# A GRU step with the state as the stationary operand and the weights streaming in four column tiles

## The chip, the cores and the metric

The kernel runs on one NeuronCore of a Trainium2 chip. The metric is the device time of one execution in microseconds. TensorE (PE in the profile), VectorE (DVE), ScalarE (ACT), GpSimd (POOL) and SyncE (SP) each run their own instruction stream in order and meet through semaphores.

## The reference

Four graph layers in a row over 1250 nodes with 512 features, each followed by a residual and a layer norm. Nearly everything the change touches is the recurrent part of the first one:

```python
def gru(x_seq, W_ih, W_hh, b_ih, b_hh):
    H = W_hh.shape[1]                       # 512
    pre_i = x_seq @ W_ih.T + b_ih           # [1250, 1536], all steps at once
    def step(h, pi):
        ph = h @ W_hh.T + b_hh              # [1536]
        r = sigmoid(pi[:H] + ph[:H])
        z = sigmoid(pi[H:2 * H] + ph[H:2 * H])
        n = tanh(pi[2 * H:] + r * ph[2 * H:])
        return (1.0 - z) * n + z * h
    # scan over the 1250 rows, h0 = 0; every h is kept
```

Each step needs the whole state of the step before, so 1250 products of a 1x512 vector with a 512x1536 matrix run one after the other.

## The kernel before

**Around the loop.** The program first builds the dense adjacency from the edge lists, runs two graph convolutions, and computes `pre_i` for all steps into `big` (line 952), seen as `pi_v`, 12 columns for each step. After the loop come the output product of this layer and the other three layers. None of that is changed but for the order of the 12 columns.

**Numbers.** State and weights are f16 pairs (high part and low part of a scaled f32), with f32 accumulation in PSUM. `whh16[g]` holds the recurrent weights of gate g (0 r, 1 z, 2 n) as two parts by four k tiles of 128x512. `h16` holds the state: which of two buffers, which half, which k of the half, and two columns (high and low part) for each.

**TensorE (lines 488 to 516).** A matmul has a 128x128 block of weights as the stationary operand and the two state columns as the moving one, so its output is two PSUM columns over 128 partitions. A gate is 4 output blocks x 4 k x 2 parts = 32 matmuls, a step is 96, each with its own weight load. The outputs are in two halves c of 256 features; each half has a PSUM bank for each gate (4c + g). Lines 501 to 516 write the order by hand: what needs only half 0 of the new state goes first (after `gru_state0`), then, after `gru_state1`, what needs half 1, with r, n and z of half 0 ahead of those of half 1. So the gates of one half are worked on by the other engines while TensorE multiplies for the other half.

**ScalarE (lines 688 to 725)** puts the step's input columns into the PSUM banks beside the products (`put`, line 691, six small copies a step) and applies the sigmoids (lines 703 and 708) and the tanh (line 712), each for one half.

**VectorE (lines 986 to 1023).** A scan (`tensor_tensor_scan`, running value times a multiplier plus the next element) over 6 or 8 PSUM elements adds high part, low part and input, undoes the scale, and for n multiplies by r (lines 988 and 994). One scan of 14 elements makes the new state and the pieces for its f16 split (line 1001). Line 1007 writes `h16` and releases TensorE; line 1009 writes the signed copy of the state into `upd_add` for the next update. All of this is per half, so there are two of each in a step.

**GpSimd (line 325)** copies the new state of a half into `r1`, which keeps all 1250. `gru_kept` and `gru_fresh` guard the next overwrite of the buffers.

All loops are written for two steps a turn (u = 0, 1; t = 2i + u).

Of the kernel before, what the change touches and what calls it, by code (L numbers as in the profile page):

```python
# [25 lines left out]
ACT = mybir.ActivationFunctionType  # L26
ALU = mybir.AluOpType
# [6 lines left out]
N, D, E = 1250, 512, 20000  # L34
P = 128
# [14 lines left out]
L2_STEPS = 35  # L50
WSLOT = KT * D


def layout(nc, io):

    ctx = ExitStack()
    with ctx:
# [35 lines left out]
        whh = [r2_f[:, 0:WSLOT], r2_f[:, WSLOT:2 * WSLOT], hn_f[:, WSLOT:2 * WSLOT]]  # L93

# [107 lines left out]
        def _(sp):  # L202
# [44 lines left out]
            for c in range(2):  # L247
                sp.wait_ge(s(f"gru_put{c}"), N + 1)
# [35 lines left out]
        def _(pool):  # L284
# [61 lines left out]
        def _(pe):  # L346
# [139 lines left out]
            every = ((0, 0), (0, 1), (1, 0), (1, 1))  # L486

            def gru_gate(u, c, kc, g, pieces=every):

                for j, k in pieces:  # L490
                    at = (4 if g == 2 else 3) * j
                    for part in range(2):
                        m = mm(psum[:, 4 * c + g, at:at + 2], whh16[g][:, part, 2 * kc + k, (2 * c + j) * P:(2 * c + j + 1) * P],  # L493
                               h16[:, u, kc, k], start=(kc == 0 and j == 0 and k == 0 and part == 0),
                               stop=(kc == 1 and k == 1 and part == 1), skip_group_check=True)
                return m

            with pe.Fori(0, N // 2) as i:
                for u in range(2):
                    t = 2 * i + u  # L500
                    pe.wait_ge(s("gru_state0"), t + 1)
                    pe.wait_ge(s("gru_put0"), t + 1)
                    for g in (0, 2, 1):
                        gru_gate(u, 0, 0, g)
                    pe.wait_ge(s("gru_put1"), t + 1)
                    gru_gate(u, 1, 0, 0)
                    gru_gate(u, 1, 0, 2, every[:1])
                    pe.wait_ge(s("gru_state1"), t + 1)
                    gru_gate(u, 0, 1, 0).then_inc(s("gru_r_mm0"), 1)
                    gru_gate(u, 0, 1, 2).then_inc(s("gru_n_mm0"), 1)  # L510
                    gru_gate(u, 0, 1, 1).then_inc(s("gru_z_mm0"), 1)
                    gru_gate(u, 1, 1, 0).then_inc(s("gru_r_mm1"), 1)
                    gru_gate(u, 1, 0, 2, every[1:])
                    gru_gate(u, 1, 1, 2).then_inc(s("gru_n_mm1"), 1)
                    gru_gate(u, 1, 0, 1)
                    gru_gate(u, 1, 1, 1).then_inc(s("gru_z_mm1"), 1)

            for c in range(2):
                pe.wait_ge(s(f"gru_kept{c}"), N + 2)
                pe.wait_ge(s(f"gru_put{c}"), N + 1)  # L520
# [115 lines left out]
        def _(act):  # L636
# [51 lines left out]
            def put(t, c, g):  # L688

                columns = psum[:, 4 * c + 2, 3:8:4] if g == 2 else psum[:, 4 * c + g, 2:6:3]  # L690
                return nc.scalar.copy(columns, big[:, bass.ds(t * 12 + c * 6 + 2 * g, 2)])  # L691

            for c in range(2):
                for g in range(2):
                    put(0, c, g)
                put(0, c, 2).then_inc(s(f"gru_put{c}"), 1)
            with act.Fori(0, N // 2) as i:
                for u in range(2):
                    t = 2 * i + u

                    def gate_r(c):
                        act.wait_ge(s(f"gru_r_sum{c}"), t + 1)
                        nc.scalar.activation(mul_n[:, c, 3:8:4], sum_rz[:, c, 0, 2:6:3], ACT.Sigmoid).then_inc(s(f"gru_r{c}"), 1)  # L703

                    def gate_z(c):

                        act.wait_ge(s(f"gru_z_sum{c}"), t + 1)
                        nc.scalar.activation(upd_mul[:, c, 2:14:7], sum_rz[:, c, 1, 2:6:3], ACT.Sigmoid).then_inc(s(f"gru_z{c}"), 1)  # L708
# [74 lines left out]
        def _(dve):  # L783
# [174 lines left out]
            link(v.memset(mul_rz[:], 1.0))  # L958
            link(v.memset(mul_rz[:, 0:6:3], 0.0))
            link(v.tensor_copy(mul_rz[:, 2:6:3], scl[:, 1:2].to_broadcast([P, 2])))  # L960
            link(v.memset(mul_n[:], 1.0))
            link(v.memset(mul_n[:, :, 0:8:4], 0.0))
            for c in range(2):
                link(v.tensor_copy(mul_n[:, c, 2:8:4], scl[:, 1:2].to_broadcast([P, 2])))
# [9 lines left out]
            for c in range(2):  # L974
                link(v.memset(psum[:, 4 * c:4 * c + 3, 0:8], 0.0))
                link(v.tensor_copy(psum[:, 4 * c + 2, 2:8:4], bhhc[:, 8 + 2 * c:10 + 2 * c]))
            dve.sem_inc(s("gru_init"), 1)
            for c in range(2):
                dve.sem_inc(s(f"gru_state{c}"), 1)
                dve.sem_inc(s(f"gru_fresh{c}"), 1)  # L980
            signs_v = signs[:].rearrange("p (j a) -> p j a", a=2)

            def sevens(ap):
                return ap.rearrange("p (j a) -> p j a", a=7)

            def scan_rz(t, c, g):
                dve.wait_ge(s(f"gru_{'rz'[g]}_mm{c}"), t + 1)
                v.tensor_tensor_scan(sum_rz[:, c, g], mul_rz[:], psum[:, 4 * c + g, 0:6], 0.0, ALU.mult, ALU.add).then_inc(s(f"gru_{'rz'[g]}_sum{c}"), 1)  # L988

            def scan_n(t, c):  # L990

                dve.wait_ge(s(f"gru_n_mm{c}"), t + 1)
                dve.wait_ge(s(f"gru_r{c}"), t + 1)
                v.tensor_tensor_scan(sum_n[:, c], mul_n[:, c], psum[:, 4 * c + 2, 0:8], 0.0, ALU.mult, ALU.add).then_inc(s(f"gru_n_sum{c}"), 1)  # L994

            def update(t, u, c):
                dve.wait_ge(s(f"gru_kept{c}"), t + 1)
                dve.wait_ge(s(f"gru_fresh{c}"), t + 1)
                for gate in "zn" if c == 0 else "nz":
                    dve.wait_ge(s(f"gru_{gate}{c}"), t + 1)  # L1000
                v.tensor_tensor_scan(upd[:, 1 - u, c], upd_mul[:, c], upd_add[:, c], 0.0, ALU.mult, ALU.add).then_inc(s(f"gru_upd{c}"), 1)  # L1001

            def parts(t, u, c):

                dve.wait_ge(s(f"gru_upd{c}"), t + 1)
                new = sevens(upd[:, 1 - u, c])
                v.tensor_tensor(h16[:, 1 - u, c], new[:, :, 3:6:2], new[:, :, 5:7], ALU.subtract).then_inc(s(f"gru_state{c}"), 1)  # L1007

                v.tensor_tensor(sevens(upd_add[:, c])[:, :, 1:3], new[:, :, 2:3].broadcast_to([P, 2, 2]), signs_v, ALU.mult).then_inc(s(f"gru_fresh{c}"), 1)  # L1009

            with dve.Fori(0, N // 2) as i:
                for u in range(2):
                    t = 2 * i + u
                    scan_rz(t, 0, 0)
                    scan_rz(t, 0, 1)
                    scan_n(t, 0)
                    scan_rz(t, 1, 0)
                    update(t, u, 0)
                    scan_n(t, 1)
                    parts(t, u, 0)  # L1020
                    scan_rz(t, 1, 1)
                    update(t, u, 1)
                    parts(t, u, 1)
# [236 lines left out]
```

## Time and profile before

| | us |
|---|---|
| median of 3 runs | 5472.36 (5461.36 to 5474.08) |
| span of the profiled execution | 5472.0 |
| TensorE matmul busy | 5225.6 (95%) |
| TensorE weight load busy | 4436.6 (81%), beside the matmuls |
| VectorE busy | 2755.6 (50%) |
| ScalarE busy | 2097.4 (38%) |
| GpSimd busy | 611.5 (11%) |
| matmuls and weight loads of line 493 | 120000 of each |

Busy time is the union of an engine's instructions; a small matmul counts from its start until its result is out (about 165 ns here), so overlapping matmuls show a busy engine whatever their rate. The rate is read from the starts. PEclk is the clock granted to TensorE, in tenths of its full 2.4 GHz (1.00 in the tables by stretch is full speed, 0.50 is 1.2 GHz).

### The profile page before, as it was taken

What the parts mean: (1) busy time and instruction counts of PE and PEld (TensorE: products, weight loads), DVE (VectorE), ACT (ScalarE), POOL (GpSimd) and SP (SyncE); (2) the same over time, 40 slices, a digit from 0 to 9 for tenths busy, and PEclk for the clock granted to TensorE, in tenths of its full rate; (3) what the DMA queues carried; (4) which work ended last, traced back from release to release, by engine and by line L of the source; (5) the groups of instructions that cost most, each with busy time, mean ns of one, the idle gap of its engine ahead of it and who ended that gap; (6) DMA issues with size and microseconds to landing.
All of it is one profiled execution on the core that took longest, in us unless ns stands there. A gap on an engine that the chain in (4) does not pass through costs nothing.

```text
span 5472.0 us, 323782 instructions
## 1 busy us (share of the span) xinstructions
PE 5225.6 (95%) x128234; PEld 4436.6 (81%) x128235; DVE 2755.6 (50%) x16453; ACT 2097.4 (38%) x15422; POOL 611.5 (11%) x2721
## 2 busy tenths in 40 slices
PE   8889999999999999999999999999999999999989
PEld 7875569999999999999999999999999744555554
DVE  5552245555555555555555555555555542554451
ACT  0110115555555555555555555555555301211110
POOL 1230001111111111111111111111111100000000
PEclk9999985555555555555555555555555699999999
DMA  1002220000000000000000000000000100000011
GB/s 57 0 9 88 77 85 0 0 0 0 0 0 0 0 0 0 0 0 0 0 0 0 0 0 0 0 0 0 0 0 0 45 10 16 34 33 19 33 40 48
DMA packets 28930, 81.07 MB, mean 15 GB/s; under 512 B 1594, under 2 KB 1834, under 8 KB 28858
## 3 DMA queue, kind: packets, MB, share of 16 engines
q1 hardware_dynamic: 28858, 80.03, 4.0%
q8 instruction: 55, 0.90, 0.1%
q14 instruction: 17, 0.14, 0.0%
HBM read 58.08 MB, written 21.95 MB: 15 GB/s over the span
## 4 chain that ended last, share of the span: by engine, by line
PE 69%; DVE 14%; ACT 7%; issue 7%; DVEq 3%; POOL 0%; DMA 0%; SPq 0%; POOLq 0%; ACTq 0%
PE psum L493 40%; PE psum L555 8%; ACT upd_mul L708 5%; PE psum L372 5%; DVE sum_rz L988 4%; DVE sum_n L994 4%; PE psum L362 4%; PE psum L567 4%; PE psum L419 4%; DVE h L1007 3%; ACT upd_add L712 2%; PE psum L479 2%; PE psum L541 2%; PE psum L631 1%; DVE upd L1001 1%
## 5 line engine op out<-in xcount | busy, mean ns | idle before, releaser
L493 PE MATMUL psum<-h,r 128*128 128x2 f16 x80000 | 2949.1, 166 | 119.8 <-ACT psum L691 4.9
L493 PEld LDWEIGHTS psum<-h,r 128*128 128x128 f16 x80000 | 2613.0, 105 | 223.9 <-DVE h L1007 218.3
L493 PE MATMUL psum<-h,hn 128*128 128x2 f16 x40000 | 1758.5, 165 | 0.2 <-issue 0.2
L493 PEld LDWEIGHTS psum<-h,hn 128*128 128x128 f16 x40000 | 1453.4, 104 | 0.3 <-issue 0.3
L988 DVE TENSOR_TENSOR_SCAN sum_rz<-mul_rz,psum 128x6 f32<-128x6 f32 x5000 | 833.8, 167 | 823.3 <-PE psum L493 823.1
L703 ACT ACTIVATE mul_n<-sum_rz 128x2 f32<-128x2 f32 x2500 | 517.5, 207 | 1409.4 <-DVE sum_rz L988 1409.4
L691 ACT COPY psum<-big 128x2 f32 (+1 forms) x7506 | 1027.7, 159 | 0.0
L1001 DVE TENSOR_TENSOR_SCAN upd<-upd_mul,upd_add 128x14 f32<-128x14 f32 x2500 | 467.0, 187 | 769.0 <-ACT upd_mul L708 460.5
L325 POOL COPY r<-upd 128x2 f32 x2500 | 469.0, 188 | 3224.8 <-DVE upd L1001 3224.8
L708 ACT ACTIVATE upd_mul<-sum_rz 128x2 f32<-128x2 f32 x2500 | 516.2, 206 | 212.4 <-DVE sum_rz L988 199.0
L712 ACT ACTIVATE upd_add<-sum_n 128x2 f32<-128x2 f32 x2500 | 495.9, 198 | 72.5 <-DVE sum_n L994 0.3
L1007 DVE TENSOR_TENSOR h<-upd 128x4 f16<-128x4 f32 x2500 | 409.9, 164 | 43.3
L994 DVE TENSOR_TENSOR_SCAN sum_n<-mul_n,psum 128x8 f32<-128x8 f32 x2500 | 423.6, 169 | 0.1
L1009 DVE TENSOR_TENSOR upd_add<-upd,signs 128x4 f32<-128x4 f32 x2500 | 391.7, 157 | 0.0
L419 PE MATMUL psum<-r 125*125 125x100 bf16 x2580 | 307.2, 309 | 16.5 <-DVE r L863 12.6
L419 PEld LDWEIGHTS psum<-r 125*125 125x125 bf16 x2580 | 286.8, 225 | 32.8 <-DVE r L863 29.0
L372 PE MATMUL psum<-adj,hn 125*128 125x417 f32 (+1 forms) x720 | 252.7, 512 | 2.1 <-ACT hn L656 1.4
L372 PEld LDWEIGHTS psum<-adj,hn 125*128 125x128 f32 x720 | 135.7, 189 | 119.6 <-issue 115.0
L555 PE MATMUL psum<-adj,r 128*125 128x512 f16 x960 | 220.7, 388 | 8.3 <-DVE r L1186 8.3
L862 DVE TENSOR_SCALAR r<-r,hn 125x1250 bf16<-125x1250 f16 x258 | 141.1, 547 | 161.8 <-issue 99.0
L555 PEld LDWEIGHTS psum<-adj,r 128*125 128x125 f16 x960 | 133.4, 139 | 89.6 <-issue 16.1
L362 PE MATMUL psum<-ws,r 128*125 128x512 f32 x400 | 181.6, 617 | 7.2 <-ACT r L730 5.9
(233 smaller groups left out, 2635.0 us busy)
## 6 DMA issues: line engine op xcount, KB each, us to landing
ws<-in_Wl SPq DMA_DIRECT2D x9, 1024.0 KB, 5.4
ws<-in_Wr SPq DMA_DIRECT2D x9, 1024.0 KB, 8.3
edge_counts<-adj SPq DMA_DIRECT2D x2, 3051.8 KB
edge_weights<-big SPq DMA_DIRECT2D x1, 6103.5 KB
adj_rows<-big SPq DMA_DIRECT2D x1, 6103.5 KB
adj<-adj_rows SPq DMA_DIRECT2D x1, 6103.5 KB
big<-edge_counts SPq DMA_DIRECT2D x1, 6103.5 KB
adj<-edge_weights SPq DMA_DIRECT2D x1, 6103.5 KB
```

The costliest lines, as they stand in the source:

```text
L372: m = mm(o[:, 0:n1 - n0], rows[0:NP, t, f * P:(f + 1) * P], mat[0:NP, t, n0:n1], start=(t == 0), stop=(t == NT - 1))
L419: m = mm(psum[0:NP, 2 * u + t // 5, (t % 5) * 100:(t % 5) * 100 + 100], src_hot[0:EP, h, t * NP:(t + 1) * NP], dst_hot[0:EP, h], start=Fal ...
L493: m = mm(psum[:, 4 * c + g, at:at + 2], whh16[g][:, part, 2 * kc + k, (2 * c + j) * P:(2 * c + j + 1) * P], h16[:, u, kc, k], start=(kc == ...
L555: m = mm(o, a(pa), b(pb), start=start and i == 0, stop=stop and i == 2)
L691: return nc.scalar.copy(columns, big[:, bass.ds(t * 12 + c * 6 + 2 * g, 2)])
L703: nc.scalar.activation(mul_n[:, c, 3:8:4], sum_rz[:, c, 0, 2:6:3], ACT.Sigmoid).then_inc(s(f"gru_r{c}"), 1)
L708: nc.scalar.activation(upd_mul[:, c, 2:14:7], sum_rz[:, c, 1, 2:6:3], ACT.Sigmoid).then_inc(s(f"gru_z{c}"), 1)
L712: nc.scalar.activation(upd_add[:, c, 0:14:7], sum_n[:, c, 3:8:4], ACT.Tanh).then_inc(s(f"gru_n{c}"), 1)
L988: v.tensor_tensor_scan(sum_rz[:, c, g], mul_rz[:], psum[:, 4 * c + g, 0:6], 0.0, ALU.mult, ALU.add).then_inc(s(f"gru_{'rz'[g]}_sum{c}"), 1)
L994: v.tensor_tensor_scan(sum_n[:, c], mul_n[:, c], psum[:, 4 * c + 2, 0:8], 0.0, ALU.mult, ALU.add).then_inc(s(f"gru_n_sum{c}"), 1)
L1001: v.tensor_tensor_scan(upd[:, 1 - u, c], upd_mul[:, c], upd_add[:, c], 0.0, ALU.mult, ALU.add).then_inc(s(f"gru_upd{c}"), 1)
L1007: v.tensor_tensor(h16[:, 1 - u, c], new[:, :, 3:6:2], new[:, :, 5:7], ALU.subtract).then_inc(s(f"gru_state{c}"), 1)
```

## The change

The operands of the recurrent matmuls trade places. The two state columns of a k tile become the stationary operand (a weight load of 2 columns), and the weights become the moving one, 128 columns a matmul. The output is two rows (high and low part of the state). Four matmuls that differ only in j write to PSUM partitions 32j and 32j + 1, each in its own column tile of 32 columns of the array, with the same state and a quarter of the gate's weights each: moving column (b, i) of tile j is output feature 128b + 32j + i. A gate is 4 k x 2 parts x 4 tiles = 32 matmuls into one bank, a step 96 as before.

The result lies in rows, and the rest of the step wants it in columns. So VectorE turns the bank with one transpose of 32x32 blocks (128 columns from PSUM) into `turned` in SBUF, four blocks of 34 entries a gate, in reversed order so that the two wanted rows land next to entries 32 and 33, where the n bias and the input stand. A scan then covers two blocks, 38 elements, most of them multiplied by zero. There are two scans a gate.

The halves are gone: one wait for the whole state, then r, n, z; one transpose and two scans for each gate; one activation for each gate over four blocks; one update scan of 28 elements; one subtraction for `h16`. `put` is one copy of 12 elements into the other buffer of `turned`, after z's sigmoid. The signed copy into `upd_add` moves from VectorE to GpSimd, ahead of the keeping copy, which now covers all four blocks.

```diff
+QR = 32
+GRP = QR + 2
+SPAN = GRP + 4
...
+        turned = hn_f[:, 2 * WSLOT:2 * WSLOT + 6 * KT * GRP].rearrange("p (u g b e) -> p u g b e", u=2, g=3, b=KT)
...
             with pool.Fori(0, N // 2) as i:
                 for u in range(2):
                     t = 2 * i + u
-                    for c in range(2):
-                        pool.wait_ge(s(f"gru_upd{c}"), t + 1)
-                        pool.tensor_copy(r1[:, 2 * c:2 * c + 2, bass.ds(t, 1)], upd[:, 1 - u, c, 2:14:7]).then_inc(s(f"gru_kept{c}"), 1)
+                    pool.wait_ge(s("gru_upd"), t + 1)
+                    new = upd[:, 1 - u].rearrange("p c (j a) -> p (c j) a", a=7)
+                    pool.tensor_tensor(upd_add[:].rearrange("p c (j a) -> p (c j) a", a=7)[:, :, 1:3], new[:, :, 2:3].broadcast_to([P, KT, 2]),
+                                       signs[:, 0:2].unsqueeze(1).broadcast_to([P, KT, 2]), ALU.mult).then_inc(s("gru_fresh"), 1)
+                    pool.tensor_copy(r1[:, :, bass.ds(t, 1)], new[:, :, 2:3]).then_inc(s("gru_kept"), 1)
...
-            def gru_gate(u, c, kc, g, pieces=every):
...
+            def gru_rows(u, g):
+
+                for k in range(KT):
                     for part in range(2):
+                        for j in range(4):
+                            w = whh16[g][:, part, k].rearrange("p (b j i) -> p b j i", j=4, i=QR)[:, :, j]
+                            o = psum[QR * j:QR * j + 2, g, 0:KT * QR].rearrange("p (b i) -> p b i", i=QR)
+                            m = mm(o, h16[:, u, k // 2, k % 2], w, start=(k == 0 and part == 0), stop=(k == KT - 1 and part == 1), skip_group_check=True)
                 return m
...
+                    pe.wait_ge(s("gru_state"), t + 1)
+                    gru_rows(u, 0).then_inc(s("gru_r_mm"), 1)
+                    gru_rows(u, 2).then_inc(s("gru_n_mm"), 1)
+                    gru_rows(u, 1).then_inc(s("gru_z_mm"), 1)
...
+            def put(t, u):
+
+                return nc.scalar.copy(turned[:, u].rearrange("p g b e -> p (g b) e")[:, :, QR + 1], big[:, bass.ds(t * 12, 12)])
...
+                    act.wait_ge(s("gru_r_sum"), 2 * t + 2)
+                    nc.scalar.activation(mul_n[:, :, 3:SPAN:GRP], sum_rz[:, :, 0, 3:SPAN:GRP], ACT.Sigmoid).then_inc(s("gru_r"), 1)
+                    act.wait_ge(s("gru_n_sum"), 2 * t + 2)
+                    nc.scalar.activation(upd_add[:, :, 0:14:7], sum_n[:, :, 3:SPAN:GRP], ACT.Tanh).then_inc(s("gru_n"), 1)
+                    act.wait_ge(s("gru_z_sum"), 2 * t + 2)
+                    nc.scalar.activation(upd_mul[:, :, 2:14:7], sum_rz[:, :, 1, 3:SPAN:GRP], ACT.Sigmoid).then_inc(s("gru_z"), 1)
+                    put(t + 1, 1 - u).then_inc(s("gru_put"), 1)
...
+            def turn_rows(t, u, g):
+                gate = "rzn"[g]
+                dve.wait_ge(s(f"gru_{gate}_mm"), t + 1)
+                v.transpose(turned[:, u, g, :, QR - 1::-1], psum[:, g, 0:KT * QR].rearrange("p (b i) -> p b i", i=QR)).then_inc(s(f"gru_{gate}_turned"), 1)
+
+            def gate_span(u, c, g):
+                at = 2 * c * GRP + QR - 2
+                return turned[:, u, g].rearrange("p b e -> p (b e)")[:, at:at + SPAN]
 
             with dve.Fori(0, N // 2) as i:
                 for u in range(2):
                     t = 2 * i + u
+                    turn_rows(t, u, 0)
+                    dve.wait_ge(s("gru_put"), t + 1)
+                    dve.wait_ge(s("gru_r_turned"), t + 1)
+                    for c in range(2):
+                        v.tensor_tensor_scan(sum_rz[:, c, 0], mul_rz[:], gate_span(u, c, 0), 0.0, ALU.mult, ALU.add).then_inc(s("gru_r_sum"), 1)
+                    turn_rows(t, u, 2)
+                    dve.wait_ge(s("gru_n_turned"), t + 1)
+                    dve.wait_ge(s("gru_r"), t + 1)
+                    for c in range(2):
+                        v.tensor_tensor_scan(sum_n[:, c], mul_n[:, c], gate_span(u, c, 2), 0.0, ALU.mult, ALU.add).then_inc(s("gru_n_sum"), 1)
+                    turn_rows(t, u, 1)
+                    dve.wait_ge(s("gru_z_turned"), t + 1)
+                    for c in range(2):
+                        v.tensor_tensor_scan(sum_rz[:, c, 1], mul_rz[:], gate_span(u, c, 1), 0.0, ALU.mult, ALU.add).then_inc(s("gru_z_sum"), 1)
+                    dve.wait_ge(s("gru_kept"), t + 1)
+                    dve.wait_ge(s("gru_fresh"), t + 1)
+                    dve.wait_ge(s("gru_z"), t + 1)
+                    dve.wait_ge(s("gru_n"), t + 1)
+                    v.tensor_tensor_scan(upd[:, 1 - u].rearrange("p c a -> p (c a)"), upd_mul[:].rearrange("p c a -> p (c a)"),
+                                         upd_add[:].rearrange("p c a -> p (c a)"), 0.0, ALU.mult, ALU.add).then_inc(s("gru_upd"), 1)
+                    dve.wait_ge(s("gru_upd"), t + 1)
+                    new = upd[:, 1 - u].rearrange("p c (j a) -> p (c j) a", a=7)
+                    v.tensor_tensor(h16[:, 1 - u].rearrange("p c k a -> p (c k) a"), new[:, :, 3:6:2], new[:, :, 5:7], ALU.subtract).then_inc(s("gru_state"), 1)
```

## Rows read from the trace of the kernel before

**Rows 1.** The span in 40 slices: busy tenths of TensorE, and its granted clock.
```profile
PE   8889999999999999999999999999999999999989
PEclk9999985555555555555555555555555699999999
```

**Rows 2.** The chain of work that ended last, shares of the span by line.
```profile
PE psum L493 40%; PE psum L555 8%; ACT upd_mul L708 5%; PE psum L372 5%; DVE sum_rz L988 4%; DVE sum_n L994 4%; PE psum L362 4%; PE psum L567 4%; PE psum L419 4%; DVE h L1007 3%; ACT upd_add L712 2%; PE psum L479 2%; PE psum L541 2%; PE psum L631 1%; DVE upd L1001 1%
```

**Rows 3.** By stretch: length, engines' busy us (instructions), granted clock, DMA share, GB/s.
```profile
200.00:300.00 100.00, 85.01 (x713) 79.80 (x713) 57.22 (x131) 15.81 (x30) 31.11 (x45) 1.00 0.00 0
...
792.00:4333.00 3541.00, 3424.53 (x119924) 3320.96 (x119921) 1907.30 (x14996) 1847.40 (x14997) 469.02 (x2500) 0.50 0.00 0
...
5328.00:5340.00 12.00, 6.10 (x23) 3.77 (x22) 6.89 (x20) 3.15 (x6) 2.74 (x5) 0.50 0.32 131
```

**Rows 4.** Timeline of one step: start us, length us, engine, line, idle before.
```profile
2002.76 0.29 PEld L493 LDWEIGHTS psum<-h,r 128*128 128x128 f16 x8 [0.17 <-DVE h L1007]
2002.91 0.21 ACT L708 ACTIVATE upd_mul<-sum_rz 128x2 f32<-128x2 f32 x1
...
2003.24 0.19 DVE L1001 TENSOR_TENSOR_SCAN upd<-upd_mul,upd_add 128x14 f32<-128x14 f32 x1 [0.37 <-ACT upd_mul L708]
2003.47 0.17 DVE L1007 TENSOR_TENSOR h<-upd 128x4 f16<-128x4 f32 x1
...
2003.90 0.17 PE L493 MATMUL psum<-h,r 128*128 128x2 f16 x1
...
2004.10 0.17 DVE L988 TENSOR_TENSOR_SCAN sum_rz<-mul_rz,psum 128x6 f32<-128x6 f32 x1 [0.40 <-PE psum L493]
...
2004.30 0.21 ACT L703 ACTIVATE mul_n<-sum_rz 128x2 f32<-128x2 f32 x1 [1.13 <-DVE sum_rz L988]
...
2004.53 0.17 DVE L988 TENSOR_TENSOR_SCAN sum_rz<-mul_rz,psum 128x6 f32<-128x6 f32 x1 [0.26 <-PE psum L493]
...
2004.61 0.17 DVE L994 TENSOR_TENSOR_SCAN sum_n<-mul_n,psum 128x8 f32<-128x8 f32 x1
...
2004.91 0.50 PEld L493 LDWEIGHTS psum<-h,r 128*128 128x128 f16 x16
...
2005.59 0.10 PEld L493 LDWEIGHTS psum<-h,r 128*128 128x128 f16 x1 [0.17 <-DVE h L1007]
```

**Rows 5.** Groups of the loop: count, busy us, mean ns of one, idle before.
```profile
L493 PEld LDWEIGHTS psum<-h,r 128*128 128x128 f16 x80000 | 2613.0, 105 | 223.9 <-DVE h L1007 218.3
...
L988 DVE TENSOR_TENSOR_SCAN sum_rz<-mul_rz,psum 128x6 f32<-128x6 f32 x5000 | 833.8, 167 | 823.3 <-PE psum L493 823.1
L703 ACT ACTIVATE mul_n<-sum_rz 128x2 f32<-128x2 f32 x2500 | 517.5, 207 | 1409.4 <-DVE sum_rz L988 1409.4
L691 ACT COPY psum<-big 128x2 f32 (+1 forms) x7506 | 1027.7, 159 | 0.0
L1001 DVE TENSOR_TENSOR_SCAN upd<-upd_mul,upd_add 128x14 f32<-128x14 f32 x2500 | 467.0, 187 | 769.0 <-ACT upd_mul L708 460.5
L325 POOL COPY r<-upd 128x2 f32 x2500 | 469.0, 188 | 3224.8 <-DVE upd L1001 3224.8
...
L1007 DVE TENSOR_TENSOR h<-upd 128x4 f16<-128x4 f32 x2500 | 409.9, 164 | 43.3
L994 DVE TENSOR_TENSOR_SCAN sum_n<-mul_n,psum 128x8 f32<-128x8 f32 x2500 | 423.6, 169 | 0.1
```

**Rows 6.** Line 1007: shortest, median and longest ns, first and last start us.
```profile
L1007 DVE TENSOR_TENSOR h<-upd x2500: 149/164/166, 792.4 to 4332.5; 128x4 f16<-128x4 f32 x193
```

**Rows 7.** Timeline of TensorE: a run of f16 matmuls of 512 columns.
```profile
4774.78 17.21 PE L555 MATMUL psum<-adj,r 128*125 128x512 f16 x79
```

**Rows 8.** VectorE copies out of PSUM, by shape.
```profile
L902 DVE COPY big<-psum 125x500 f32<-125x500 f32 x20 | 12.5, 665 | 90.0 <-PE psum L461 90.0
...
L902 DVE COPY big<-psum 125x250 f32<-125x250 f32 x10 | 4.0, 404 | 0.0
```

**Rows 9.** Line 401: weight loads of a single column.
```profile
L401 PEld LDWEIGHTS psum<-ident,hn x4: 76/98/119, 11.5 to 11.6; 50*1 50x1 f32 x4
```

More of the change, by code:

```diff
@@ L316, in _ @@
             pool.partition_all_reduce(wmax[:, 7:8], wmax[:, 6:7], P, bass.bass_isa.ReduceOp.max).then_inc(s("top_all"), 1)
-            for c in range(2):
-                pool.sem_inc(s(f"gru_kept{c}"), 2)
+            pool.sem_inc(s("gru_kept"), 2)
             with pool.Fori(0, N // 2) as i:
@@ L500, in _ @@
                     t = 2 * i + u
[L501 to L520, printed above, removed]
+                    pe.wait_ge(s("gru_state"), t + 1)
+                    gru_rows(u, 0).then_inc(s("gru_r_mm"), 1)
+                    gru_rows(u, 2).then_inc(s("gru_n_mm"), 1)
+                    gru_rows(u, 1).then_inc(s("gru_z_mm"), 1)
+            pe.wait_ge(s("gru_kept"), N + 2)
             pe.wait_ge(s("wfc_in"), 16)
@@ L686, in _ @@
             nc.scalar.activation(warm[:], scl[:, 1:2], ACT.Sigmoid).then_inc(s("warm"), 1)
[L688 to L696, printed above, removed]
+            def put(t, u):
+                return nc.scalar.copy(turned[:, u].rearrange("p g b e -> p (g b) e")[:, :, QR + 1], big[:, bass.ds(t * 12, 12)])
+            put(0, 0).then_inc(s("gru_put"), 1)
             with act.Fori(0, N // 2) as i:
@@ L957, in _ @@
             link(v.memset(h16[:], 0.0))
[L958 to L962, printed above, removed]
+            link(v.memset(turned, 0.0))
+            link(v.memset(mul_rz[:], 0.0))
+            link(v.memset(mul_n[:], 0.0))
+            for at in (1, 3):
+                link(v.memset(mul_rz[:, at:SPAN:GRP], 1.0))
+            link(v.memset(mul_n[:, :, 1:SPAN:GRP], 1.0))
+            link(v.tensor_copy(mul_rz[:, 2:SPAN:GRP], scl[:, 1:2].to_broadcast([P, 2])))
             for c in range(2):
-                link(v.tensor_copy(mul_n[:, c, 2:8:4], scl[:, 1:2].to_broadcast([P, 2])))
+                link(v.tensor_copy(mul_n[:, c, 2:SPAN:GRP], scl[:, 1:2].to_broadcast([P, 2])))
+            for u in range(2):
+                link(v.tensor_copy(turned[:, u, 2, :, QR], bhhc[:, 8:12]))
             link(v.memset(upd_mul[:], 1.0))
@@ L973, in _ @@
             link(v.memset(signs[:, 0:4:2], -1.0))
-            for c in range(2):
-                link(v.memset(psum[:, 4 * c:4 * c + 3, 0:8], 0.0))
-                link(v.tensor_copy(psum[:, 4 * c + 2, 2:8:4], bhhc[:, 8 + 2 * c:10 + 2 * c]))
+            link(v.memset(psum[:, 0:6, 0:KT * QR], 0.0))
             dve.sem_inc(s("gru_init"), 1)
[L978 to L1009, printed above, removed]
+            dve.sem_inc(s("gru_state"), 1)
```

51 lines of the change are left out of this document (7 added, 44 removed).

## The prediction

> **What bounds the kernel now.** I read the 40 slices first. From about 0.8 ms to 4.3 ms TensorE is 90% busy or more, and its granted clock is half of full speed [rows 1]. This is the GRU loop, 3541 us of 5472.0 [rows 3], and the chain of work that ended last goes mostly through its matmul line 493 [rows 2]. The diff touches only this loop and its setup, so the rest, 5472.0 - 3541 = 1931 us, stays.
>
> The 2500 operations of line 1007 (two per step) start from 792.4 to 4332.5 us [rows 6]: 3540.1 / 1249.5 = 2.833 us per step. The timeline of one step shows how it fills [rows 4]. Sixteen weight loads of 104 ns each take 0.50 us, so one starts every (0.50 - 0.104) / 15 = 0.0264 us [rows 4, 5]. A step has 96 pairs of weight load and matmul. TensorE waits once a step for the first half of the new state, 0.17 us from the end of the load before [rows 4]; from start to start that is 0.17 + 0.104 = 0.27, of which 0.25 is beyond the pace. (2.833 - 0.25) / 96 = 0.0269. I use 0.0267, between the two: 96 x 0.0267 = 2.56 us. So the step is bound by TensorE, by the rate at which 128x128 weights enter the array. ScalarE, VectorE and the rest of the chain lie almost wholly under it, because the two halves of the state alternate.
>
> **The change, part by part.** The number of pairs stays 96 (3 gates x 4 k x 2 parts x 4 column tiles), but the weight load now has 2 columns and the matmul streams 128. The halves are gone, so everything between the last matmul of the z gate and the first of the next step is exposed. The step is TensorE's time plus that tail.
>
> *TensorE.* No row has two column tiles at work. At full clock, 79 f16 matmuls of 512 columns take 17.21 us, last one 0.39: 0.216 us each, 0.421 ns per column [rows 7]. So 128 columns take 54 ns at 2.4 GHz and 107 ns at 1.2 GHz. Floor: four tiles side by side, a pair every 107 / 4 = 26.7 ns at 1.2 GHz, or 54 / 4 = 13.5 at 2.4. Ceiling: one after the other, 107 or 54 ns a pair. The nearest row for the issue of pairs is the loop itself, 26.7 ns a pair [rows 4, 5]; no row shows a shorter one. I take 26.7 ns, which is both what four tiles give at 1.2 GHz and what is shown to issue: 96 x 0.0267 = 2.56 us, no gain over now.
>
> *The clock.* With 2 moving columns a matmul it stayed at 0.50 through the loop [rows 3]. It was 1.00 where line 419 streams 100 columns a matmul with gaps, and 0.50 in a late stretch where TensorE is busy only half the time [rows 3]. The new loop streams 128 columns and idles for 1.8 us a step, between these two, so either level is possible. With 26.7 ns a pair set by issue, it changes the matmul's own latency only (-0.05 us a step, -65 us in all).
>
> *The tail,* link by link. A link is one start to the dependent start.
> - Last matmul to VectorE: 0.203 now (2003.90 to 2004.10) [rows 4], plus 126 more columns at 1.2 GHz, 0.105: 0.308 (0.256 at 2.4).
> - New 32x32 transpose of 128 elements from PSUM. Copies from PSUM take 404 ns at 250 elements and 665 at 500 [rows 8], 1.044 ns an element plus 143, so 277 at 128. Bounds 0.277 to 0.404; I take 0.30, near the copy and a little up for filling the block. To its reader, as from line 1001 to 1007 (0.22 less 0.187) [rows 4, 5]: 0.035. Sum 0.335.
> - Two scans of 38 elements in place of 6. 6, 8 and 14 elements take 167, 169 and 187 ns [rows 5], 1.3 to 2.9 ns an element: 0.208 to 0.256, I take 0.235. The second starts 0.08 after the first for short ones [rows 4]; with 30 more elements 0.125 to 0.175, I take 0.14. Sum 0.375.
> - VectorE to ScalarE 0.034 (2004.10 to 2004.30 less 0.167), sigmoid 0.206 [rows 4, 5]: 0.240. One activation now covers four blocks; 2 more elements cost nothing visible.
> - Sigmoid end to the update scan: 2002.91 + 0.206 to 2003.24 [rows 4]: 0.13. It waits on four semaphores.
> - Update scan of 28 elements instead of 14: 187 + 14 x (1.3 to 2.9) = 0.205 to 0.227, with its link 0.035: 0.250.
> - State subtraction (0.164 [rows 5], four more elements) and the first load after it: 0.18.
>
> Sum 0.308 + 0.335 + 0.375 + 0.240 + 0.13 + 0.250 + 0.18 = 1.818 us. The step is 2.56 + 1.82 = 4.38 us. The loop grows by (4.38 - 2.833) x 1250 = 1934 us, the kernel to 5472 + 1934 = 7406, rounded 7400. With all links at their ends the step lies between 4.22 and 4.55, so 7200 to 7620. The span equals the median of the runs (5472.36), so nothing is added.
>
> *What costs nothing.* r and n on VectorE: r's matmuls end at 0.85, its transpose can start at 1.16 and its scans end at 1.87, before n's matmuls have arrived at 2.01; n's scans end near 2.7, and z's transpose waits for z's matmuls until 2.87. Cover left 0.15 us; if it is gone, the tail grows by the excess. The input columns: six ScalarE copies of 0.159 a step become one of 12 elements behind z's sigmoid [rows 5]; it needs to land only before the next step's r scans, over a microsecond later. VectorE waits for it ahead of r's scans, with n's transpose queued behind. GpSimd now issues the signed copy of the state (was VectorE's, line 1009) and then the keeping copy (0.188 [rows 5]); both have until the next update, 4 us away. If VectorE's subtraction beside them were slowed by sharing memory ports, up to 0.2 us a step would come on the tail. Setup (a few memsets, other strides for the inputs) runs once: under 5 us.
>
> *Against the skill.* The loop shows a weight load every 26.7 ns beside matmuls in flight [rows 4, 5]. The Trainium skill (TensorEngine Tiling (Array Packing), Instruction Overhead) gives each matmul about 60 cycles however few its columns. As an estimate, that is 25 ns at 2.4 GHz: by it the loop's matmuls would need 2.4 us, not 2.56, even at the high clock, and the 13.5 ns rival below could not occur. I keep that rival at a lower chance.
>
> **Rivals.**
> - *B, high clock and fast issue.* If the clock rises and pairs issue every 13.5 ns, a gate takes 0.43 us and TensorE 1.28. Then VectorE's own in-order chain binds: r arrives at 0.68, its sigmoid ends at 1.63, n's scans start at 1.73, z's transpose at 2.01, its scans end at 2.72, sigmoid and wait to 3.09, update and state to 3.52. Step 3.52: 5472 + 0.687 x 1250 = 6330. For: the 26.7 ns of now is the pace of 128-column loads, not proven to be the issue's. Against: no row issues faster.
> - *C, weight loads come on top.* Four tiles run together, but each round of four also pays its small load. One-column loads show 76 to 119 ns, median 98 [rows 9]. A round is 54 + 98 = 152 ns at 2.4 GHz: 24 rounds 3.65, plus a tail of about 1.77, step 5.4, 8700 us; at 1.2 GHz a round of 205 ns gives a step of 6.74, 10350. For: no row shows small loads beside matmuls in column tiles. Against: loads hide under matmuls everywhere in this trace [rows 4]. The Trainium skill (TensorE: Matmul & The Clock Gate, The mechanism, in the part on packing small matmuls) says a load overlaps a matmul in flight only where the row groups differ, and all four tiles here share theirs; today's loop, with the same row groups throughout, does not bear it out.
> - *D, the change does not do what it says.* The tiles are not concurrent: 96 x 54 ns = 5.18 us, plus 1.77, step 6.95: 5472 + 4.12 x 1250 = 10620 at 2.4 GHz; at 1.2 GHz 10.27 + 1.82 gives 17040. For: nothing here shows concurrency. Against: nothing either, the outputs go to disjoint partitions.
> - *E, faster.* VectorE is the place: B's issue rate, and VectorE's links overlap as short ones do now (0.08 apart) instead of ending first. The step beats 2.833 only if 0.69 us leaves B's chain, which has two exposed transposes and two scan pairs on it: all four at 0.18 instead of 0.335 and 0.375 takes 0.70 away. With 0.1 more from the waits the step is 2.72: 5330 us. Against: a dependent operation waits for its producer's end in every row here.
>
> **How the numbers follow.** A 0.52 (7400; 7200 to 7620), B 0.20, C 0.12 (0.08 of it at the high clock), D 0.12, E 0.03, no change 0.01. The range from 6200 to 8900 takes in A, B and C at the high clock: 0.80. A measurement of this kernel can tell about 0.3% from no change; slower by more has 0.96, within 0.01, faster 0.03. The sign is firm because even the best TensorE leaves a serial chain above 2.833 us.
>
> **What the profile will show.** The loop should last 1250 x 4.38 = 5475 us. If TensorE is right, a gate's 32 matmuls span 0.85 us and TensorE then idles 1.8 us less the latency of its last matmul. B shows gates of 0.43 us, a clock of 1.00 and VectorE at the end of the chain throughout; C about 0.15 or 0.2 us between rounds of four; D gates of 1.7 or 3.4 us. The transposes should take 0.28 to 0.40 us, the scans 0.21 to 0.26. I am wrong if TensorE's gates don't keep to the pace of 26.7 ns a pair, or if VectorE is no longer idle when z's matmuls arrive.

## The result, and the profile after

The changed kernel takes 6795.86 us (median of 4 runs, 6793.9 to 6800.4); the kernel before takes 5469.49 in the same comparison. The ratio is 1.2432, 95% interval 1.2416 to 1.2447: slower, by 1326 us. The profiled execution has a span of 6794.0 us.

The page of the changed kernel, in 40 slices, answers [rows 1]. Busy tenths of TensorE and VectorE, and the granted clock:

```profile
PE   8899744444444444444444444444444448999998
DVE  5542455555555555555555555555555555254552
PEclk9999988888888888888888888888888889989999
```

TensorE is no longer busy for most of the loop, and its clock reads 0.8 where it was 0.5. Neither level of the clock is 0.8. By stretch (length; PE, PEld, DVE, ACT, POOL busy; granted clock), against [rows 3]:

```profile
792.00:5653.00 4861.00, 2344.46 (x119840) 2057.84 (x119828) 2841.58 (x13735) 918.26 (x4996) 415.72 (x2496) 0.81 0.00 0
...
2995.00:3005.00 10.00, 6.34 (x252) 5.62 (x240) 5.93 (x28) 1.68 (x9) 0.67 (x4) 0.52 0.00 0
3007.00:3021.00 14.00, 5.88 (x384) 5.13 (x372) 8.47 (x42) 2.91 (x16) 1.00 (x6) 1.00 0.00 0
```

The loop went from 3541 to 4861 us; the other stages stayed. Inside it, stretches at full clock follow stretches at half clock. So there are two kinds of step. From the starts of the state's subtraction, 897 steps take 3.69 us and 352 take 4.42. Against 2.833 that is 897 x 0.856 + 352 x 1.582 = 1325 us, the whole difference.

One step at half clock, in the timeline (start, length, engine, line, idle before), to be read against [rows 4]:

```profile
3002.42 0.73 PEld L498 LDWEIGHTS psum<-r,h 128*2 128x2 f16 x32 [1.98 <-DVE h L983]
3002.42 1.02 PE L498 MATMUL psum<-r,h 128*2 128x128 f16 x32 [1.69 <-DVE h L983]
3003.12 0.89 PEld L498 LDWEIGHTS psum<-hn,h 128*2 128x2 f16 x32
...
3003.50 0.32 DVE L952 STREAM_TRANSPOSE hn<-psum 128x128 f32<-128x128 f32 x1 [1.13 <-PE psum L498]
...
3003.98 0.88 PEld L498 LDWEIGHTS psum<-r,h 128*2 128x2 f16 x32
3004.08 1.07 PE L498 MATMUL psum<-r,h 128*2 128x128 f16 x32
...
3004.70 0.36 DVE L970 TENSOR_TENSOR_SCAN sum_n<-mul_n,hn 128x38 f32<-128x38 f32 x2
...
3005.21 0.32 DVE L952 STREAM_TRANSPOSE hn<-psum 128x128 f32<-128x128 f32 x1
3005.56 0.36 DVE L974 TENSOR_TENSOR_SCAN sum_rz<-mul_rz,hn 128x38 f32<-128x38 f32 x2
3005.95 0.21 ACT L691 ACTIVATE upd_mul<-sum_rz 128x4 f32<-128x4 f32 x1 [0.64 <-DVE sum_rz L974]
...
3006.36 0.22 DVE L979 TENSOR_TENSOR_SCAN upd<-upd_mul,upd_add 128x28 f32<-128x28 f32 x1 [0.44 <-ACT upd_mul L691]
3006.61 0.17 DVE L983 TENSOR_TENSOR h<-upd 128x8 f16<-128x8 f32 x1
...
3006.84 0.43 PEld L498 LDWEIGHTS psum<-r,h 128*2 128x2 f16 x32 [1.98 <-DVE h L983]
```

Gates follow each other at 0.86 us (3003.12 to 3003.98), 26.7 ns a pair. n's scans are done at 3005.06, z's matmuls end at 3005.15, z's transpose starts at 3005.21: VectorE has been waiting for TensorE. From there to the next step's first load (3006.84) nothing overlaps: 1.69 us.

And one step at full clock:

```profile
3014.22 0.43 PEld L498 LDWEIGHTS psum<-r,h 128*2 128x2 f16 x32 [2.37 <-DVE h L983]
...
3014.61 0.48 PEld L498 LDWEIGHTS psum<-hn,h 128*2 128x2 f16 x32
...
3014.89 0.32 DVE L952 STREAM_TRANSPOSE hn<-psum 128x128 f32<-128x128 f32 x1 [0.72 <-PE psum L498]
3015.05 0.48 PEld L498 LDWEIGHTS psum<-r,h 128*2 128x2 f16 x32
3015.11 0.62 PE L498 MATMUL psum<-r,h 128*2 128x128 f16 x32
3015.31 0.37 DVE L965 TENSOR_TENSOR_SCAN sum_rz<-mul_rz,hn 128x38 f32<-128x38 f32 x2
3015.59 0.29 DVE L952 STREAM_TRANSPOSE hn<-psum 128x128 f32<-128x128 f32 x1
3015.71 0.21 ACT L687 ACTIVATE mul_n<-sum_rz 128x4 f32<-128x4 f32 x1 [2.06 <-DVE sum_rz L965]
3016.02 0.36 DVE L970 TENSOR_TENSOR_SCAN sum_n<-mul_n,hn 128x38 f32<-128x38 f32 x2
3016.30 0.29 DVE L952 STREAM_TRANSPOSE hn<-psum 128x128 f32<-128x128 f32 x1
3016.41 0.21 ACT L689 ACTIVATE upd_add<-sum_n 128x4 f32<-128x4 f32 x1 [0.50 <-DVE sum_n L970]
...
3017.02 0.21 ACT L691 ACTIVATE upd_mul<-sum_rz 128x4 f32<-128x4 f32 x1 [0.40 <-DVE sum_rz L974]
```

A gate takes 0.44 us (3014.61 to 3015.05), 13.9 ns a pair. z's matmuls are done at 3015.73, but VectorE comes to z's transpose only at 3016.30, 0.57 us later. TensorE is not what the step waits for any more, except for the r gate at its start. From r's transpose on it is VectorE's work in order, with one wait in it for ScalarE: n's transpose ends at 3015.88, r's sigmoid at 3015.92, and n's scans start at 3016.02.

### The profile page after: what moved, and what is told of

Read it like the earlier page. It is cut to its first block, busy times and chain, and to the rows that moved or that the text cites. A ratio compares the mean times of both kernels' runs of the same rounds, so it can differ in the third digit from the quotient of the medians.

```text
span 6794.0 us, 302521 instructions
## 1 busy us (share of the span) xinstructions
PE 4145.8 (61%) x128234; PEld 3175.1 (47%) x128235; DVE 3694.9 (54%) x15204; ACT 1168.0 (17%) x5417; POOL 558.8 (8%) x2721
## 4 chain that ended last, share of the span: by engine, by line
issue 72%; PE 19%; POOL 5%; DVE 2%; POOLq 1%; DVEq 1%; ACT 0%; DMA 0%; SPq 0%; ACTq 0%
PE psum L544 6%; POOL r L330 3%; PE psum L556 3%; PE psum L424 3%; PE psum L367 2%; POOL upd_add L328 2%; PE psum L530 1%; PE psum L377 1%; PE psum L620 1%; POOLq L330 1%; POOLq L323 1%; DVE r L830 0%; PE psum L434 0%; DVEq L823 0%; DVEq L822 0%
## 5 line engine op out<-in xcount | busy, mean ns | idle before, releaser
L498 PE MATMUL psum<-r,h 128*2 128x128 f16 x80000 | 1879.0, 247 | 2523.3 <-DVE h L983 2517.0
L498 PEld LDWEIGHTS psum<-r,h 128*2 128x2 f16 x80000 | 1405.5, 95 | 2810.6 <-DVE h L983 2803.6
L952 DVE STREAM_TRANSPOSE hn<-psum 128x128 f32<-128x128 f32 x3750 | 1143.8, 305 | 1120.6 <-PE psum L498 1048.4
L498 PE MATMUL psum<-hn,h 128*2 128x128 f16 x40000 | 933.6, 245 | 0.0
L498 PEld LDWEIGHTS psum<-hn,h 128*2 128x2 f16 x40000 | 747.1, 96 | 0.0
L687 ACT ACTIVATE mul_n<-sum_rz 128x4 f32<-128x4 f32 x1250 | 262.5, 210 | 2713.5 <-DVE sum_rz L965 2713.5
L979 DVE TENSOR_TENSOR_SCAN upd<-upd_mul,upd_add 128x28 f32<-128x28 f32 x1250 | 270.9, 217 | 553.9 <-ACT upd_mul L691 553.9
L970 DVE TENSOR_TENSOR_SCAN sum_n<-mul_n,hn 128x38 f32<-128x38 f32 x2500 | 455.8, 224 | 134.9
L965 DVE TENSOR_TENSOR_SCAN sum_rz<-mul_rz,hn 128x38 f32<-128x38 f32 x2500 | 456.7, 225 | 128.5
L974 DVE TENSOR_TENSOR_SCAN sum_rz<-mul_rz,hn 128x38 f32<-128x38 f32 x2500 | 455.7, 223 | 42.5
L691 ACT ACTIVATE upd_mul<-sum_rz 128x4 f32<-128x4 f32 x1250 | 262.7, 210 | 583.7 <-DVE sum_rz L974 583.7
```

What stands on the lines that cost most here:

```text
L498: m = mm(o, h16[:, u, k // 2, k % 2], w, start=(k == 0 and part == 0), stop=(k == KT - 1 and part == 1), skip_group_check=True)
L691: nc.scalar.activation(upd_mul[:, :, 2:14:7], sum_rz[:, :, 1, 3:SPAN:GRP], ACT.Sigmoid).then_inc(s("gru_z"), 1)
L952: v.transpose(turned[:, u, g, :, QR - 1::-1], psum[:, g, 0:KT * QR].rearrange("p (b i) -> p b i", i=QR)).then_inc(s(f"gru_{gate}_turned"), 1)
L965: v.tensor_tensor_scan(sum_rz[:, c, 0], mul_rz[:], gate_span(u, c, 0), 0.0, ALU.mult, ALU.add).then_inc(s("gru_r_sum"), 1)
L970: v.tensor_tensor_scan(sum_n[:, c], mul_n[:, c], gate_span(u, c, 2), 0.0, ALU.mult, ALU.add).then_inc(s("gru_n_sum"), 1)
L974: v.tensor_tensor_scan(sum_rz[:, c, 1], mul_rz[:], gate_span(u, c, 1), 0.0, ALU.mult, ALU.add).then_inc(s("gru_z_sum"), 1)
```

## The experiments

Three questions were open. Do the four column tiles really run together? What does the clock cost, and what does VectorE's chain? And which part of the change loses the time: the swap of the operands, or the end of the overlap between the halves? All loops below start at about 0.79 ms and the rest of the kernel is unchanged, so a step is read from the subtraction's starts.

**One column tile for all four.**

```diff
-                            o = psum[QR * j:QR * j + 2, g, 0:KT * QR].rearrange("p (b i) -> p b i", i=QR)
+                            o = psum[0:2, g, 0:KT * QR].rearrange("p (b i) -> p b i", i=QR)
```

> The changed kernel, but the four matmuls of a round all use column tile 0 and write the same two PSUM rows (each overwrites or adds to the others, so three quarters of each gate are lost). Counts and shapes of all instructions stay. Theory 1, four column tiles stream side by side and only the streamed columns set the pace: a gate's 32 matmuls now take 32 x 54 = 1.7 us at full clock, the step 5.2 + 1.8 = 7.0 us, the kernel about 10600 us (17000 at half clock). Rival, the pace is that of issuing or of small weight loads and the tiles don't matter: gate and time unchanged, about 6800 us.

Measured: 10918 us (one run). Line 498 in the timeline:

```profile
3001.08 1.76 PEld L498 LDWEIGHTS psum<-r,h 128*2 128x2 f16 x32 [1.86 <-DVE h L983]
...
3002.81 1.81 PEld L498 LDWEIGHTS psum<-hn,h 128*2 128x2 f16 x32
...
3004.59 1.81 PEld L498 LDWEIGHTS psum<-r,h 128*2 128x2 f16 x32
```

A gate takes 1.78 us (3002.81 to 3004.59), 55.6 ns a pair, at a clock of 1.00 throughout, and the step 7.19 us. In four tiles the same pairs take 13.9 ns: the tiles run side by side, at a quarter of the time to within 1%. My rival D (10620 us at full clock) would have looked like this.

**32 streamed columns instead of 128.**

```diff
-                            w = whh16[g][:, part, k].rearrange("p (b j i) -> p b j i", j=4, i=QR)[:, :, j]
-                            o = psum[QR * j:QR * j + 2, g, 0:KT * QR].rearrange("p (b i) -> p b i", i=QR)
+                            w = whh16[g][:, part, k].rearrange("p (b j i) -> p b j i", j=4, i=QR)[:, 0:1, j]
+                            o = psum[QR * j:QR * j + 2, g, 0:QR].rearrange("p (b i) -> p b i", i=QR)
```

> The changed kernel with 32 streamed columns a matmul in place of 128 (three of four feature blocks are left out), same count of pairs. It shows how fast pairs can be issued. If streamed columns alone set the pace, a round of four starts every 27 ns at half clock or 13 at full, and a gate takes 0.21 or 0.11 us; if a pair needs 13.4 ns to issue, a gate keeps 0.43 us; if 26.7 ns, 0.85 us. Theory, VectorE's in-order chain binds once TensorE is fast: the step loses only what the r gate loses, 3.69 - 0.22 = 3.47 us, the kernel about 6270 us. Rival, TensorE's gates still bind: the step loses 0.65 us or more, below 5750 us. The granted clock should be 0.50 throughout if it goes by streamed columns.

Measured: 6303 us (one run), step 3.50 us. By stretch, and in the timeline:

```profile
800.00:5168.00 4368.00, 1213.79 (x119808) 1049.09 (x119808) 2763.97 (x13729) 917.43 (x4992) 415.08 (x2496) 0.50 0.00 0
```

```profile
3002.50 0.25 PEld L498 LDWEIGHTS psum<-r,h 128*2 128x2 f16 x32 [2.66 <-DVE h L983]
...
3002.68 0.36 PEld L498 LDWEIGHTS psum<-hn,h 128*2 128x2 f16 x32
...
3002.98 0.32 DVE L952 STREAM_TRANSPOSE hn<-psum 128x128 f32<-128x128 f32 x1 [0.54 <-PE psum L498]
```

Two things follow. The n gate's 32 loads of 0.079 us take 0.36 us, so a pair is issued every (0.36 - 0.079) / 31 = 9 ns; the r gate's, right behind the wait for the state, come every (0.25 - 0.079) / 31 = 5.5 ns. The n gate's 0.32 us (3002.68 to 3003.00) lies between the values that I had named, 0.21 and 0.43. All this is at half clock; no run shows how close pairs come at full clock. The 26.7 ns of the kernel before was not a pace of issue. And at half clock, with three quarters of TensorE's streaming gone, the step is only 0.19 us shorter than the changed kernel's at full clock. That is the r gate alone: from the first load to r's transpose 0.48 us (3002.50 to 3002.98) instead of 0.67 (3014.22 to 3014.89). VectorE's chain binds, as the theory had it (6270 expected). The clock stayed at 0.50 in the whole loop.

**Filler matmuls behind the z gate.**

```diff
                     gru_rows(u, 1).then_inc(s("gru_z_mm"), 1)
+                    for _ in range(2):
+                        gru_rows(u, 1, 7)
```

(The third argument is the bank.)

> The changed kernel with 64 more matmuls after the z gate (the z gate twice more, into a bank that nobody reads), in the time in which TensorE waits for the state. Theory, the half-speed stretches (352 of 1249 steps at 4.41 us beside 897 at 3.69) come from TensorE idling, and cost 352 x 0.72 = 253 us: granted clock 1.00 through the loop, every step 3.69 us, the kernel 6544 us. Rival, the clock goes by something else: it still alternates, and the time is 6796 us or, where the filler at half clock (1.7 us) delays the next step, more.

Measured: 6539.88 us (ratio to before 1.1961, interval 1.1941 to 1.1981). All 1249 steps take 3.69 us, and the clock stays up:

```profile
800.00:5400.00 4600.00, 2993.96 (x199272) 2760.77 (x199262) 2760.07 (x13701) 917.77 (x4983) 414.82 (x2492) 1.00 0.00 0
```

TensorE is busy 65% of this stretch (2994 of 4600), against 42% in the full-clock stretch of the changed kernel (5.88 of 14 us), which ended in a fall to half clock. The half-clock steps cost 6796 - 6540 = 256 us, where 253 was expected. The rival, a clock that still alternates, did not come.

**The kernel before, whole gates.** TensorE's part of the edit; the others follow the same order.

```diff
                     pe.wait_ge(s("gru_put0"), t + 1)
+                    pe.wait_ge(s("gru_put1"), t + 1)
+                    pe.wait_ge(s("gru_state1"), t + 1)
                     for g in (0, 2, 1):
...
+                        for c in range(2):
+                            gru_gate(u, c, 0, g)
+                            gru_gate(u, c, 1, g).then_inc(s(f"gru_{'rzn'[g]}_mm{c}"), 1)
```

> The kernel before with its operands as they were (weights stationary), but without the overlap of the halves: TensorE waits for both halves of the state, then does the whole r, n and z gates, and the other engines take both halves of each gate one after the other. Theory, the loss of the change is the loss of the overlap: TensorE 2.56 us plus an exposed tail of 0.20 + 0.25 + 0.34 + 0.13 + 0.31 + 0.25 = 1.5 us, step 4.0 us, the kernel about 6950 us, slower than the changed one. Rival, the swap of operands (transposes, long scans) is what costs: then without the halves this kernel stays near its old time, at most 0.3 us a step more, below 5850 us.

Measured: 6721.36 us (ratio 1.2294, interval 1.2273 to 1.2314). The step is 3.84 us, all at half clock:

```profile
3001.37 0.94 PEld L493 LDWEIGHTS psum<-h,r 128*128 128x128 f16 x32 [1.19 <-DVE h L999]
...
3002.23 0.93 PEld L493 LDWEIGHTS psum<-h,hn 128*128 128x128 f16 x32
...
3003.09 0.93 PEld L493 LDWEIGHTS psum<-h,r 128*128 128x128 f16 x32
```

The same 26.7 ns a pair as before, and from the last load's end to the next step's first 1.19 us in which TensorE has nothing to do. This kernel has neither transposes nor long scans nor column tiles, and still loses 1.01 us a step (3.84 - 2.833), nearly all that the change loses (1.06 on average). The rival is excluded. My terms add to 2.56 + 1.48 = 4.04 us, 0.20 too long, nearly all of it in the tail (3.84 - 2.56 = 1.28 us beside the matmuls). It is 75 us faster than the changed kernel, not slower.

**Order r, z, n and early waits.** VectorE's part (the order changes on all three engines):

```diff
+                    dve.wait_ge(s("gru_kept"), t + 1)
+                    dve.wait_ge(s("gru_fresh"), t + 1)
+                    dve.wait_ge(s("gru_r"), t + 1)
+                    turn_rows(t, u, 2)
+                    dve.wait_ge(s("gru_z"), t + 1)
+                    dve.wait_ge(s("gru_n_turned"), t + 1)
...
+                    dve.wait_ge(s("gru_n"), t + 1)
```

> The changed kernel in the order r, z, n in place of r, n, z on all engines, and with the update's waits for GpSimd and for z moved ahead of n's scans, so that only the wait for the tanh stands before the update scan. Same instructions. Theory: the wait for r's sigmoid before n's scans (0.08 us) goes at full clock because z's transpose and scans lie there, and the link from ScalarE to the update shrinks from 0.20 us (end of sigmoid to start of update scan) to about 0.04, at either clock. Steps 3.45 us at full clock and 4.25 at half; with the same share of slow steps about 6530 us. Rival, the waits are not worth anything in themselves: only the 0.08 us of 900 steps, about 6720 us.

Measured: 6522.07 us, the median of four runs of 6468, 6502, 6542 and 6586 us; the ratio, 1.1904 (1.1848 to 1.196), is that of the first three. In the profiled execution (6467.8) 1060 steps take 3.49 us and 189 take 4.42. So the full-clock step lost 0.20 us (0.24 expected), but the half-clock step nothing, where 0.16 was expected; the kernel's time came out near the forecast because fewer steps were slow (189, not 352). The sum was right for a wrong reason.

The end of a half-clock step shows where the gain went:

```profile
3005.68 1.07 PE L498 MATMUL psum<-hn,h 128*2 128x128 f16 x32
...
3006.90 0.32 DVE L952 STREAM_TRANSPOSE hn<-psum 128x128 f32<-128x128 f32 x1 [0.23 <-PE psum L498]
3007.32 0.36 DVE L977 TENSOR_TENSOR_SCAN sum_n<-mul_n,hn 128x38 f32<-128x38 f32 x2
3007.72 0.21 ACT L691 ACTIVATE upd_add<-sum_n 128x4 f32<-128x4 f32 x1 [0.81 <-DVE sum_n L977]
...
3007.96 0.22 DVE L979 TENSOR_TENSOR_SCAN upd<-upd_mul,upd_add 128x28 f32<-128x28 f32 x1 [0.28 <-ACT upd_add L691]
```

The last link is 0.24 us (3007.72 to 3007.96), where the changed kernel has 0.41 (3005.95 to 3006.36): 0.17 gained. But the last gate's matmuls end at 3006.75 and its transpose starts 0.15 us later, where it was 0.06, and its scans follow 0.42 us after that, where it was 0.35: 0.16 lost. At half clock the last transpose waits for TensorE, so the waits moved in front of it and of its scans lie on the path again. At full clock VectorE comes late to that transpose, and what stands in front of it adds nothing: the link to the update gives 0.17; the middle gate's scans start about 0.10 earlier behind their transpose (0.32 us in place of 0.43), no longer waiting for r's sigmoid; the last scans give back 0.07 (0.39 in place of 0.32). Together that is 0.20.

The four runs differ by the clock: their mean granted clocks over the whole execution are 0.921, 0.908, 0.896 and 0.881, from the shortest to the longest. Why the share of half-clock steps varies so much here, and hardly in the changed kernel (0.860 or 0.861 in all four runs), no run shows.

**The same with the filler.** The 64 matmuls stand behind n, now the last gate.

> The order and the early waits, and the 64 filler matmuls behind the last gate. Theory: every step at full clock, 3.45 us, the kernel 1931 + 4313 = 6245 us, still 14% slower than the kernel before, since VectorE's chain (three transposes, six scans, update, subtraction) and not TensorE sets the step. Rival: TensorE is late too, and then the order brings nothing beyond the filler: 6540 us.

Measured: 6288.51 us, ratio 1.1508 (1.1492 to 1.1525), step 3.49 us. The end of a step:

```profile
3003.70 0.29 DVE L954 STREAM_TRANSPOSE hn<-psum 128x128 f32<-128x128 f32 x1
3003.82 0.21 ACT L691 ACTIVATE upd_mul<-sum_rz 128x4 f32<-128x4 f32 x1 [0.40 <-DVE sum_rz L971]
3004.10 0.36 DVE L979 TENSOR_TENSOR_SCAN sum_n<-mul_n,hn 128x38 f32<-128x38 f32 x2
3004.50 0.21 ACT L693 ACTIVATE upd_add<-sum_n 128x4 f32<-128x4 f32 x1 [0.46 <-DVE sum_n L979]
...
3004.74 0.22 DVE L981 TENSOR_TENSOR_SCAN upd<-upd_mul,upd_add 128x28 f32<-128x28 f32 x1 [0.28 <-ACT upd_add L693]
```

From the last activation to the update scan it is again 0.24 us (3004.50 to 3004.74) in place of 0.41: 0.17 us for the place of three of the four waits. The clock is 1.00 from 800 to 5150 us (expected: 3.45 us a step, 6245 us), and the rival, 6540, is excluded. This is the fastest form with the operands swapped, and it is still 15% slower than the kernel before.

**Only one scan for each gate, with the filler** (`for c in range(1)` in all three places, and ScalarE's waits for the sums count one scan a step).

> The changed kernel with the filler, and with only the first of the two scans of each gate (the other half of the features gets no sums; that half of the computation is left out). Theory, at full clock VectorE's in-order chain binds from the r gate on, with all three pairs of scans on it: the second scan starts 0.14 us after the first, so 3 x 0.14 = 0.42 us go, step 3.27 us, the kernel about 6015 us. Rival, TensorE's gates bind until z is done and only z's scans are exposed: 0.14 us go, step 3.55, about 6365 us.

Measured: 6059 us (one run), step 3.31 us. Against the filler alone (3.69) 0.385 us are gone. The first load and the three activations of a step:

```profile
3001.40 0.43 PEld L498 LDWEIGHTS psum<-r,h 128*2 128x2 f16 x32 [1.09 <-DVE h L987]
...
3002.76 0.21 ACT L689 ACTIVATE mul_n<-sum_rz 128x4 f32<-128x4 f32 x1 [1.93 <-DVE sum_rz L969]
3003.35 0.21 ACT L691 ACTIVATE upd_add<-sum_n 128x4 f32<-128x4 f32 x1 [0.37 <-DVE sum_n L974]
3003.83 0.21 ACT L693 ACTIVATE upd_mul<-sum_rz 128x4 f32<-128x4 f32 x1 [0.27 <-DVE sum_rz L978]
```

From the first load they start 1.36, 1.95 and 2.43 us later; in the full-clock step of the changed kernel (first load 3014.22) it is 1.49, 2.19 and 2.80. So each gate gives about 0.13 us, what its second scan costs (I had 0.14), and the three add up. With only z's scans exposed one would have. The chain through VectorE holds all three gates.

**The kernel before, whole gates, with a filler** of two 512-column matmuls a step.

> The kernel before without the overlap of the halves, plus two matmuls of 512 columns a step behind the z gate (results unused), in TensorE's idle time, to raise its granted clock. Theory: the pace of 26.7 ns is that of loading 128x128 weights and does not depend on the granted clock, so even if the clock comes to 1.00 a gate keeps its 0.85 us and the time stays near 6721 us (less at most 50 us from the last matmul's latency). Rival: the pace halves with the clock at 2.4 GHz, a gate takes 0.43 us, the step loses over 1 us, below 5500 us. If the clock stays at 0.50 nothing is told.

Measured: 6733 us (one run), and the clock stayed at 0.50 through the loop. It tells nothing on whether the pace of weight loads follows the clock.

## Why the prediction was right, and where not

The range and the sign held. The time, 6796, lies between my case A (7400) and case B (6330), and outside the bounds of A, to which I gave 0.52 (7200 to 7620). It is inside the range because that was drawn from 6200 to 8900 to hold A, B and C; that much of it is the width of the range, not the sizing.

- **TensorE, and the step that failed.** I took 26.7 ns a pair for all steps, because no row showed a shorter one. It was right at half clock, where four tiles of 128 columns give it, and wrong at full clock, where pairs come every 13.9 ns. Issue allows 9 ns or less even at half clock. So in 72% of the steps TensorE's pace did not bind as A has it. The reading that failed was to take the pace of 128x128 loads in [rows 4, 5] for the nearest row to the issue of pairs. I named that doubt under B and gave it 0.20.
- **The clock.** I wrote that either level is possible and let each case have one. The loop has both, 1.8 ms at half and 3.1 ms at full clock. The half-clock step of A came out at 4.42 (4.38 predicted), the full-clock step of B at 3.69 (3.52 predicted). Weighted by the steps at each clock, the two forecasts give 5472 + 897 x 0.687 + 352 x 1.547 = 6633, 163 us short of the result, nearly all of it B's 0.17 us a step. What made 7400 too long is both: I did not expect a mixture of clocks, and I let the high clock change only a matmul's latency (-65 us), because I took the pace for that of issue.
- **The tail.** From the end of z's matmuls I had 1.818 - 0.27 = 1.55 us, measured 1.69. The transpose with its link (0.335; 0.35 measured) and the scans with theirs (0.409; 0.39) were right. Too small were the sigmoid with the four waits behind it (0.34; 0.41) and the last link to the first load (0.18; 0.23). TensorE's part was 0.10 too long (2.83 with the last latency; 2.73), so that the step of A is right to 0.04 us in part because two errors cancel. B was short by the same two links and by one more: from r's transpose to its scans it is 0.42 us (3014.89 to 3015.31), where I had 0.335. The wait for the input columns stands there, and z's, without it, take 0.35; that the wait is the cause is likely, but no run moved it.
- **What costs nothing.** At half clock r and n were hidden, as said. At full clock they were not, as B said: the z transpose starts 0.57 us after z's matmuls end. GpSimd's two operations are done long before the next update, and the input copy before the next r scans. The subtraction beside GpSimd's copy took 0.169 us on average (0.164 before, with half the elements): of the 0.2 us that I feared there nothing came.
- **The other rivals.** D is excluded by the run with one tile, E by every step measured (3.69 us at the least, and 2.833 was to be beaten). C, that small loads come on top of each round, is excluded too: a round takes 4 x 13.9 = 55.6 ns, what one tile needs for 128 columns. The rule of the Trainium skill (TensorE: Matmul & The Clock Gate, The mechanism) that a load overlaps a matmul in flight only where the row groups differ does not hold for these tiles: all share their row groups, and loads of 95 ns (mean) start every 13.9 ns beside matmuls in flight. Nor does the one of about 60 cycles for each matmul in the Trainium skill (TensorEngine Tiling (Array Packing), Instruction Overhead): as an estimate that is 25 ns at 2.4 GHz and 50 at 1.2, and 13.9 and 9 ns a pair were measured.
- **What I did not separate.** I charged the whole loss to the tail that the swap exposes. The whole-gate run shows where it comes from: giving up the halves alone costs 1.01 us a step. Against that kernel (3.84 us a step) the swap costs 0.58 at half clock (4.42) and gains 0.15 at full clock (3.69), which is 0.05 more on average. Whether matmuls with the weights stationary would also go faster at full clock is open; no run brought that kernel to it. Not tried: the swapped operands with halves. Nothing here says what they would give, except that VectorE, busy 2762 of 4350 us in the fastest form (2.2 us a step), would have little room below the 2.83 us of the kernel before.

## What to carry to other kernels

In a loop whose steps depend on each other, look first at what overlaps: here the overlap of two halves was worth 1.0 us of a 2.8 us step, more than matmuls at twice the pace gave back. Before speeding up the engine that binds, add up the in-order work of the next one (three transposes, six scans and two more a step) from the trace. A pace in a trace is that of its own operands (128x128 loads), not a floor for other shapes; keep it as a bound, not as the value.

## What the runs showed of the hardware that I had not expected

- The granted clock can alternate inside one steady loop: with 128-column matmuls it went up and down for 4.9 ms (steps of 3.69 and 4.42 us); TensorE was busy 42% of a stretch at full clock (5.88 of 14 us) and 63% of one almost wholly at half (6.34 of 10). Matmuls whose results nobody reads, in the idle time, held it at 1.00 and saved 256 us. With 32-column matmuls it stayed at 0.50.
- Four column tiles gave a quarter of the time of one, 13.9 against 55.6 ns a pair.
- Pairs of a load of 2 columns and a matmul of 32 were issued every 9 ns at half clock, and every 5.5 ns right after a wait.
- Moving three waits from in front of the update to in front of an earlier transpose took 0.17 us off the link to the update at either clock. Where that transpose waits for TensorE (half clock) the same waits cost 0.16 us there, and the step gained nothing; at full clock, with the new order of the gates, it gained 0.20.
